# Ternary weights w1 and w2 from one ScalarE sign instead of a ScalarE relu and a VectorE clip

## The chip, the cores and the metric
One core of one Trainium2 chip runs the whole program. The metric is device time in microseconds (us), the median of three runs of the kernel. Beside it stands one execution taken by the hardware profiler; all rows below come from that one.

## What is computed
The input x is 2 x 2048 x 512 in float32. One layer attends from x to a context of 128 rows (8 heads), adds the projected result times a gate, and applies a feed-forward part with ternary weights `w_fc` (2048 x 512) and `w_proj` (512 x 2048) and a squared relu. A second layer mixes each row with `W` and applies a feed-forward part whose weights w1 (2048 x 512) and w2 (512 x 2048) are ternary too. For the change only this matters, from the second feed-forward part:

```python
def weight_quant(w):
    scale = 1.0 / jnp.clip(jnp.mean(jnp.abs(w)), 1e-05)
    q = jnp.clip(jnp.round(w * scale), -1.0, 1.0) / scale
    return w + jax.lax.stop_gradient(q - w)
```

The kernel holds w1 and w2 as the integers -1, 0 and 1 in 8-bit floats and puts the scale into the row factors of the activations. The clip of an integer to [-1, 1] and its sign are the same number.

## The kernel before, in words
The rows of x go through the kernel in 16 groups of 256 (`GROUPS`), each in two tiles of 128. TensorE does all products and, at the start, transposes of weights; ScalarE does exp, gelu, squares, copies and the high halves of split operands; VectorE does maxima, norms, drains of PSUM and the low halves; GpSimd (POOL) does low halves and adds; SyncE issues the loads and the transposing DMAs.

The order of the work is written out by hand: for each engine a table (`ORDER` for what is done per group, `PREP` for what is done once) gives each operation its place in that engine's sequence, and the engine goes through the places in turn. Between engines there are only semaphores. An engine that waits holds up all that stands behind it.

The weights are made ready once, in the first 200 us, between the operations of groups 0, 1 and 2. For w1 and w2 this goes in eight pieces of 128 x 2048 float32 (four of w1, then four of w2), after a first pass over the same data that takes their mean:

- SyncE loads piece n (n = 0 to 7) into one of two places, both in the tile `h` (`load`, lines 599 and 601). A load waits until the piece that was there has been used (`used`).
- VectorE rounds it in place: times the inverse mean, plus MAGIC (12582912.0), which leaves MAGIC plus an integer (`round_weights`, line 1158, semaphore `c_round`).
- ScalarE lifts it: relu of the piece plus (1 - MAGIC), that is max(integer + 1, 0), into a bf16 buffer `lifted[n % 2]`, which lies in `hT` (line 932, `c_lift`). From n = 2 on it waits until clip n - 2 has left the buffer.
- VectorE clips it: min with 2, minus 1, as an 8-bit float into `w1T` or `w2T` (`clip_weights`, line 1173, `c_clip`). Before the first piece of w1 it waits for the products that read `w1T`'s memory as another weight (`c_cps`), before the first of w2 for the split of `wx` (`c_whi`, `c_wlo`), whose source lies in `w2T`.

TensorE waits for `c_clip` at its first product with w1 (4 pieces) and with w2 (8 pieces), SyncE at the first transpose into `hT` (8 pieces). The similar weights `w_fc` and `w_proj` are made by TensorE transposes and a ScalarE Sign from PSUM with the bias `drop` = -MAGIC (line 874).

Other lines that the prediction speaks of: 1365 (VectorE, the low half of a split, here of probabilities `p`, queries and attention output `qT`), 1391, 1395 and 1399 (VectorE: row maximum, bias of the exp, inverse of the sum), 949 (ScalarE exp), 957 (ScalarE, high half of the probabilities), 971 and 975 (ScalarE, the low-rank path to `tlow`), 985, 990 and 996 (ScalarE, drain of the first feed-forward part: relu and squares), 1130 (VectorE, low half of `wx`), 1417 (VectorE, residual after attention), 1430 (VectorE, remainder of the low-rank path), 759 and 764 (POOL, low half of the hidden values, and norm of the probabilities), 617 (SyncE, transposing DMA of `p` into `pt`), 1758 (TensorE, probabilities times values), 1818, 1844, 1887 and 1903 (TensorE: up, down, w1, w2).

Of the kernel before, what the change touches and what calls it, by code (L numbers as in the profile page):

```python
# [19 lines left out]
ACT = mybir.ActivationFunctionType  # L20
# [3 lines left out]
P = 128  # L24
# [24 lines left out]
def build(nc, x_d, ctxT_d, wqT_d, wkvT_d, woT_d, wfc_d, wproj_d, uT_d, wxT_d, wcT_d, bx_d, w1T_d, b1_d, w2T_d, b2_d,  # L49
          rope_d, small_d, out_d):  # L50
    ctx = ExitStack()
    with ctx:
# [32 lines left out]
        lift = sb("lift", [P, 1], F32)  # L85
# [140 lines left out]
        def mix_bank(g, n):  # L226
# [15 lines left out]
        lifted = [hT[:, t, :, :].rearrange("p c n -> p (c n)").bitcast(BF16) for t in range(TILES)]  # L242
# [18 lines left out]
         c_scps, c_sc, c_asum, c_asumps, c_mean, c_round, c_lift, c_clip) = [sem(n) for n in (  # L261
# [4 lines left out]
            "c_asumps c_mean c_round c_lift c_clip").split()]  # L266
# [55 lines left out]
        def used(eng, n):  # L322

            if n < SUM0:
                eng.wait_ge(c_tern, KC * (n + 1))
            elif n < W0:
                eng.wait_ge(c_asum, n - SUM0 + 1)
            else:
                eng.wait_ge(c_lift, n - W0 + 1)

        def last_in(place):
# [49 lines left out]
                rot_lo=((26, 28), (68, 71), (112, 113), (164, 165), (213, 214), (263, 264), (310, 311), (357, 360),  # L381
                        (409, 410), (457, 458), (505, 506), (553, 554), (604, 605), (653, 654), (703, 704),
                        (751, 752)),
                rot=((19, 21), (65, 66), (110, 111), (160, 163), (210, 212), (259, 260), (306, 307), (356, 358),
                     (407, 408), (453, 454), (503, 504), (551, 552), (600, 601), (649, 650), (701, 702), (744, 745)),
                sum=((35, 38, 42, 43), (77, 84, 85, 93), (118, 120, 130, 135), (168, 172, 179, 181),
# [3 lines left out]
                max=((30, 32, 33, 37), (74, 75, 78, 79), (115, 116, 121, 122), (166, 167, 170, 173),  # L390
# [3 lines left out]
                p_lo=((40, 41, 46, 49), (83, 89, 95, 96), (127, 136, 137, 141), (174, 178, 186, 187),  # L394
# [3 lines left out]
                pv=((53, 54), (99, 101), (144, 145), (191, 192), (239, 240), (290, 291), (338, 339), (386, 387),  # L398
                    (433, 434), (484, 486), (536, 537), (584, 585), (634, 635), (681, 683), (730, 731), (779, 780)),
                x1=((57, 59), (105, 106), (149, 150), (195, 196), (247, 248), (294, 295), (342, 344), (390, 391),  # L400
                    (439, 440), (491, 492), (540, 541), (588, 591), (639, 640), (687, 688), (737, 738), (783, 787)),
                ln2=((58, 64), (108, 109), (152, 153), (197, 198), (250, 251), (297, 298), (346, 347), (392, 393),
                     (445, 446), (496, 497), (546, 547), (593, 595), (644, 645), (689, 690), (739, 741), (784, 791)),
                low=((82,), (117,), (159,), (207,), (258,), (308,), (355,), (403,), (455,), (507,), (555,), (603,),
                     (651,), (697,), (749,), (796,)),
                q4=((123, 126), (171, 176), (215, 233), (262, 279), (317, 322), (363, 378), (411, 431), (463, 474),
                    (516, 521), (565, 576), (614, 619), (658, 665), (708, 716), (757, 766), (795, 798), (819, 821)),
                x3=((119, 124), (162, 175), (211, 221), (257, 272), (312, 321), (361, 375), (405, 422), (459, 468),
                    (513, 520), (558, 566), (606, 615), (655, 664), (699, 713), (753, 765), (793, 797), (818, 820)),
                h=((131, 132, 133, 134, 138, 139, 143, 147), (180, 183, 184, 185, 188, 190, 202, 206),  # L410
# [7 lines left out]
                q5_sc=((140, 156), (189, 208), (238, 253), (289, 303), (334, 352), (384, 404), (432, 450),  # L418
                       (483, 499), (534, 545), (580, 596), (631, 646), (680, 691), (726, 746), (775, 786),
                       (803, 809), (828, 833)),  # L420
                q5=((142, 158), (193, 209), (241, 256), (292, 305), (340, 359), (389, 406), (437, 452), (485, 502),
                    (538, 548), (583, 599), (632, 647), (682, 700), (736, 748), (781, 788), (805, 812), (832, 834)),
                x4=((154, 169), (203, 216), (254, 266), (304, 316), (351, 369), (399, 416), (451, 462), (500, 515),
                    (550, 562), (598, 609), (642, 657), (692, 705), (747, 758), (790, 794), (816, 824), (835, 836)),
                ln3=((104, 107), (148, 161), (199, 204), (246, 261), (301, 309), (343, 354), (388, 402), (438, 456),
                     (490, 501), (544, 557), (590, 602), (638, 652), (686, 696), (732, 750), (785, 792), (811, 815)),
                x2=((100, 103), (146, 157), (194, 200), (237, 255), (293, 302), (341, 353), (385, 397), (436, 449),
                    (487, 498), (539, 549), (587, 597), (637, 648), (684, 694), (725, 740), (782, 789), (810, 813)),
                ln1_st=((0, 1), (10, 12), (60, 61), (125, 151), (177, 201), (223, 249), (280, 296), (333, 345),
                        (376, 396), (426, 441), (469, 493), (527, 542), (567, 592), (623, 641), (685, 695),  # L430
                        (727, 728)),
                ln1=((2, 3), (11, 15), (63, 69), (128, 155), (182, 205), (227, 252), (288, 300), (335, 348),
                     (383, 398), (435, 444), (480, 495), (532, 543), (572, 594), (633, 643), (693, 698), (733, 734))),
# [99 lines left out]
            DVE=dict(x3lo_end=(814, 817), ctx_sum=(14,), rot_k=(8, 9), wq_max=(4,), wq_scale=(5,), k_max=(16,),  # L533
# [3 lines left out]
                     wx_lo=(88,), row_scale=(62,), mean=(70,), diag=(56,), round=(72, 73, 81, 86, 90, 91, 98, 102),  # L537
                     clip=(76, 80, 87, 92, 94, 97, 114, 129)),
# [40 lines left out]
        def _(sp):  # L579
# [260 lines left out]
        def _(act):  # L840
# [18 lines left out]
            def evac(q):  # L859

                kind, i = QUANT[q]
                if q == 0:
                    act.wait_ge(c_const, 6)
# [217 lines left out]
        def _(dve):  # L1081
# [78 lines left out]
            def clip_weights(n):  # L1160
# [827 lines left out]
```

## Time and profile before

| | us |
|---|---|
| median of 3 runs | 1144.55 (1144.29 to 1144.96) |
| the profiled execution: its own time | 1145.46 |
| its span in the profile | 1143.4 |
| TensorE busy | 1086.2 (95%) |
| VectorE busy | 923.9 (81%) |
| ScalarE busy | 798.3 (70%) |
| GpSimd busy | 584.6 (51%) |

The span goes from the first to the last instruction that the profiler recorded; the execution's own time has 2.1 us around it. Busy time is the time in which an engine had an instruction under way, and says nothing of whether others waited for it.

### The profile page before, as it was taken

What the parts mean: (1) busy time and instruction counts of PE and PEld (TensorE: products, weight loads), DVE (VectorE), ACT (ScalarE), POOL (GpSimd) and SP (SyncE); (2) the same over time, 40 slices, a digit from 0 to 9 for tenths busy, and PEclk for the clock granted to TensorE, in tenths of its full rate; (3) what the DMA queues carried; (4) which work ended last, traced back from release to release, by engine and by line L of the source; (5) the groups of instructions that cost most, each with busy time, mean ns of one, the idle gap of its engine ahead of it and who ended that gap; (6) DMA issues with size and microseconds to landing.
All of it is one profiled execution on the core that took longest, in us unless ns stands there. A gap on an engine that the chain in (4) does not pass through costs nothing.

```text
span 1143.4 us, 22172 instructions
## 1 busy us (share of the span) xinstructions
PE 1086.2 (95%) x8270; PEld 676.6 (59%) x8558; DVE 923.9 (81%) x1989; ACT 798.3 (70%) x1575; POOL 584.6 (51%) x567
## 2 busy tenths in 40 slices
PE   5776799999999999999999999999999999999997
PEld 5544556475756656474756656565756666564744
DVE  3786788988788797878889888888878777988676
ACT  3988957677685949485876849495775868595634
POOL 1442646564655655556546457463546466564421
PEclk9988799999999999999999999999999999999998
DMA  9779751452534443433335245334343254333110
GB/s 335 239 241 317 232 147 41 95 130 65 120 79 103 98 105 86 100 82 87 93 83 139 61 112 97 86 101 87 89 99 99 54 109 114 75 93 74 38 47 28
DMA packets 273802, 128.11 MB, mean 112 GB/s; under 512 B 247568, under 2 KB 248080, under 8 KB 272016
## 3 DMA queue, kind: packets, MB, share of 16 engines
q1 hardware_dynamic: 273136, 125.73, 43.6%
q8 instruction: 67, 1.10, 0.4%
q10 hardware_dynamic: 560, 0.96, 0.3%
q14 instruction: 39, 0.32, 0.1%
HBM read 57.19 MB, written 8.39 MB: 57 GB/s over the span
## 4 chain that ended last, share of the span: by engine, by line
PE 86%; DMA 4%; ACT 3%; DVE 3%; issue 1%; SPq 1%; POOL 1%; ACTq 0%; DVEq 0%
PE ps L1844 19%; PE ps L1818 18%; PE ps L1887 10%; PE ps L1903 9%; PE ps L1866 7%; PE ps L1771 6%; PE ps L1718 6%; PE ps L1824 2%; PE ps L1758 2%; PE ps L1743 2%; DMA w1T<-in_wcT 1%; PE ps L1611 1%; DMA hT<-q 1%; PE ps L1683 1%; PE ps L1660 1%
## 5 line engine op out<-in xcount | busy, mean ns | idle before, releaser
L1818 PE MATMUL ps<-xT,fcT 128*128 128x256 f16 x2048 | 259.1, 274 | 8.2 <-DMA xT<-x16f 3.9
L732 POOL TENSOR_TENSOR rs<-ve,nhalf 128x1 f32<-128x1 f32 x160 | 102.1, 643 | 283.1 <-DVE ve L1357 207.9
L1844 PE MATMUL ps<-pjT,hid 128*128 128x512 fp8e4 x1024 | 232.1, 379 | 0.0
L1818 PEld LDWEIGHTS ps<-xT,fcT 128*128 128x128 fp8e4 x2048 | 199.1, 98 | 47.1 <-issue 6.5
L759 POOL TENSOR_TENSOR hid<-sq,hid 128x512 f16<-128x512 f32 x128 | 158.6, 1246 | 49.8 <-ACT sq L996 49.3
L1844 PEld LDWEIGHTS ps<-pjT,hid 128*128 128x128 f16 x1024 | 98.3, 98 | 98.9
L949 ACT ACTIVATE e<-ps,nmb,sig 128x128 f32<-128x128 f32 x256 | 113.0, 458 | 7.9 <-DVE nmb L1395 7.8
L985 ACT ACTIVATE rl<-ps,rsf 128x256 f32<-128x256 f32 x256 | 106.5, 469 | 15.6 <-PE ps L1824 14.9
L1887 PE MATMUL ps<-w1T,q4T 128*128 128x512 fp8e4 x480 | 113.4, 379 | 0.0
L764 POOL TENSOR_TENSOR e<-e,einv 128x512 f32<-128x512 f32 x64 | 71.0, 1116 | 74.2 <-DVE einv L1399 73.9
L1903 PE MATMUL ps<-w2T,hT 128*128 128x512 fp8e4 x480 | 108.6, 379 | 0.3 <-DMA hT<-q 0.3
L1503 DVE SCALAR_TENSOR_TENSOR h<-ps,dqs,b1bc 128x512 f32<-128x512 f32 x120 | 86.4, 743 | 21.1 <-PE ps L1887 19.8
L1041 ACT ACTIVATE q<-h 128x2048 f16<-128x2048 f32 x30 | 57.2, 1908 | 55.3 <-DVE h L1514 55.3
L1718 PE MATMUL ps<-pt,wq 128*128 128x256 f16 x768 | 88.2, 275 | 3.6 <-DMA pt<-x16a 2.7
L1771 PE MATMUL ps<-wo,qT 128*128 128x512 f16 x384 | 85.6, 379 | 1.0 <-DVE qT L1365 1.0
L1718 PEld LDWEIGHTS ps<-pt,wq 128*128 128x128 f16 x768 | 75.4, 99 | 16.9 <-DMA pt<-x16a 3.5
L990 ACT ACTIVATE hid<-rl 128x512 f16<-128x512 f32 x128 | 80.7, 630 | 5.0
L1866 PE MATMUL ps<-wx,xT 128*128 128x512 f16 x360 | 82.4, 379 | 1.4 <-DVE r L1539 1.3
L1083 DVE TENSOR_REDUCE amax<-h 128x1 f32<-128x2048 f32 x30 | 68.5, 2282 | 15.3 <-ACT h L1010 15.3
L996 ACT ACTIVATE sq<-rl 128x512 f32<-128x512 f32 x128 | 78.5, 613 | 0.0
L1903 PEld LDWEIGHTS ps<-w2T,hT 128*128 128x128 f16 x480 | 45.9, 98 | 50.6
L1824 PE MATMUL ps<-tlow,lowA 128*128 128x256 bf16 x256 | 68.2, 273 | 0.1
(243 smaller groups left out, 1987.6 us busy)
## 6 DMA issues: line engine op xcount, KB each, us to landing
xb<-in_x SPq DMA_DIRECT2D x16, 512.0 KB, 4.3
xa<-in_x SPq DMA_DIRECT2D x15, 512.0 KB, 3.9
out<-r SPq DMA_DIRECT2D x30, 256.0 KB, 2.3
rope<-in_rope SPq DMA_DIRECT2D x16, 384.0 KB, 3.5
h<-in_w1T SPq DMA_DIRECT2D x6, 1024.0 KB, 6.4
h<-in_w2T SPq DMA_DIRECT2D x6, 1024.0 KB, 5.9
hid<-in_w_fc SPq DMA_DIRECT2D x2, 1024.0 KB, 8.7
h<-in_wkvT SPq DMA_DIRECT2D x2, 1024.0 KB, 10.3
```

The source lines that it names most:

```text
L732: pool.tensor_tensor(rs[:, n, t:t + 1], ve[:, n, t:t + 1], nhalf[:, :], ALU.pow).then_inc(done, 1)
L759: pool.tensor_tensor(flat[:, 1, :], sq[:, m % 2, :], flat[:, 0, :], ALU.subtract).then_inc(hid_lo, 1)
L949: last = act.activation(e[:, n, a * S:(a + 1) * S], s_bank(g, n)[:, a * S:(a + 1) * S], ACT.Exp, bias=nmb[:, n, a:a + 1], scale=sig[:, :], ...
L985: act.activation(rl[:, m % 2, a * G:(a + 1) * G], ps[:, FFN0 + m % 2, a * G:(a + 1) * G], ACT.Relu, scale=rsf[:, 2 * m + a:2 * m + a + 1]) ...
L1718: mm = pe.matmul(q_bank(hg)[:, a * G:(a + 1) * G], wq[:, ws, k, c:c + P], xT1[:, xs, k, :], start=(n == 0 and k == 0), stop=(n == 2 and k ...
L1771: mm = pe.matmul(wo_bank(t), ao[:, xs, k, t * P:(t + 1) * P], wo[:, ws, k, :], start=(n == 0 and k == 0), stop=(n == 2 and k == KC - 1))
L1818: pe.matmul(ps[:, FFN0 + m % 2, a * G:(a + 1) * G], fcT[:, k, f * P:(f + 1) * P], xT2[:, xs, k, :], start=(xs == 0 and k == 0), stop=False)
L1824: return pe.matmul(ps[:, FFN0 + m % 2, a * G:(a + 1) * G], lowA[:, f * P:(f + 1) * P], tlow[:, :], start=False, stop=True)
L1844: mm = pe.matmul(ps[:, FFN0 + t, :], hid[:, xs, c, t * P:(t + 1) * P], pjT[:, c, :], start=(c == 0 and xs == 0), stop=(c == FC - 1 and xs ...
L1866: mm = pe.matmul(mix_bank(g, t), xT3_of(g)[:, xs, k, t * P:(t + 1) * P], wx[:, ws, k, :], start=(n == 0 and k == 0), stop=(n == 2 and k == ...
L1887: mm = pe.matmul(mix_bank(g, 2 + u), q4T_of(g)[:, k, t * P:(t + 1) * P], w1T[:, k, n * 512:(n + 1) * 512], start=(k == 0), stop=(k == KC - 1))
L1903: mm = pe.matmul(mix_bank(g, 10 + t), hT_of(g)[:, t, c, :], w2T[:, c, :], start=(c == 0), stop=(c == FC - 1))
```

## The change
Piece n is still rounded by VectorE. ScalarE then takes the sign of (piece - MAGIC) and writes it straight into `w1T` or `w2T`; VectorE's clip, the buffers `lifted`, the constant `lift` and the wait of ScalarE for the clip are gone. The waits that stood before the clips of pieces 0 and 4 now stand before ScalarE's signs of these pieces, and the waits for `c_clip` are waits for `c_tern12`, which the sign raises; SyncE's first transpose into `hT` waits for the mean's sums (`used(sp, last_in(4))`) instead. The places in VectorE's table are renumbered without the eight clips, and nothing else in them changes its turn; the tables of the other engines are as they were.

```diff
-                    if n >= 2:
-                        act.wait_ge(c_clip, n - 1)
+                    kind, i = LOADS[W0 + n]
+                    if kind == "w1":
+                        if i == 0:
+                            act.wait_ge(c_cps, BATCH)
+                        dst = w1T[:, i, :]
                     else:
-                        used(act, last_in(4))
-                    act.activation(lifted[n % 2], piece[PLACE[W0 + n]], ACT.Relu, bias=lift[:, :]).then_inc(c_lift, 1)
+                        if i == 0:
+                            act.wait_ge(c_whi, 3)
+                            act.wait_ge(c_wlo, 3)
+                        dst = w2T[:, 4 * i:4 * i + 4, :].rearrange("p c n -> p (c n)")
+                    act.activation(dst, piece[PLACE[W0 + n]], ACT.Sign, bias=drop[:, :], saturate=False).then_inc(c_tern12, 1)
...
-            def clip_weights(n):
-
-                kind, i = LOADS[W0 + n]
-                dve.wait_ge(c_lift, n + 1)
-                if kind == "w1":
-                    if i == 0:
-                        dve.wait_ge(c_cps, BATCH)
-                    dst = w1T[:, i, :]
-                else:
-                    if i == 0:
-                        dve.wait_ge(c_whi, 3)
-                        dve.wait_ge(c_wlo, 3)
-                    dst = w2T[:, 4 * i:4 * i + 4, :].rearrange("p c n -> p (c n)")
-                dve.tensor_scalar(dst, lifted[n % 2], 2.0, 1.0, ALU.min, ALU.subtract, saturate=False)\
-                    .then_inc(c_clip, 1)
...
-                for n in here("DVE", "clip", p):
-                    clip_weights(n)
...
-            pool.memset(lift[:, :], 1.0 - MAGIC).then_inc(c_const, 1)
...
                 if first(g) and t == 0:
-                    sp.wait_ge(c_clip, 8)
+                    used(sp, last_in(4))
                 need(sp, w2_ps, TILES, g - 1, t)
```

## Rows read from the trace of the kernel before

**Rows 1.** The page: busy time, share of the span and instructions of each engine.

```profile
PE 1086.2 (95%) x8270; PEld 676.6 (59%) x8558; DVE 923.9 (81%) x1989; ACT 798.3 (70%) x1575; POOL 584.6 (51%) x567
```

**Rows 2.** Busy time by stretch: PE, PEld, DVE, ACT, POOL (instructions), clock, DMA share, GB/s.

```profile
107.90:144.40 36.50, 23.90 (x252) 18.39 (x253) 26.14 (x35) 35.41 (x76) 20.38 (x14) 0.72 0.80 244
144.40:181.00 36.60, 34.94 (x300) 19.60 (x309) 28.50 (x51) 17.98 (x29) 15.68 (x15) 1.00 0.51 130
181.00:1080.00 899.00, 895.28 (x6953) 554.67 (x7208) 750.34 (x1636) 635.72 (x1271) 497.94 (x479) 1.00 0.40 91
```

**Rows 3.** TensorE's waits, 117 to 220 us: total us, times, longest.

```profile
PE ps L1818 <- DVE tres L1430: 2.5, 2, 1.7
...
PE ps L1718 <- DVE r L1417: 0.9, 1, 0.9
PE ps L1771 <- DVE qT L1365: 0.5, 1, 0.5
```

**Rows 4.** All waits of ScalarE, 107.9 to 152.3 us.

```profile
ACT rl L985 <- PE ps L1824: 0.6, 1, 0.6
ACT lowsum L971 <- PE ps L1784: 0.3, 1, 0.3
```

**Rows 5.** Groups by line and form, first 200 us: busy us, mean ns | idle before.

```profile
L949 ACT ACTIVATE e<-ps,nmb,sig 128x128 f32<-128x128 f32 x43 | 19.0, 460 | 0.0
...
L932 ACT ACTIVATE hT<-h,lift 128x2048 bf16<-128x2048 f32 x8 | 15.9, 1994 | 0.0
...
L874 ACT ACTIVATE pjT<-ps,drop 128x512 fp8e4<-128x512 f32 x16 | 10.1, 685 | 1.4 <-PE ps L1611 1.4
...
L924 ACT ACTIVATE h<-h 128x2048 f32<-128x2048 f32 x4 | 7.6, 1905 | 4.1 <-DMA h<-in_w2T 4.1
...
L1173 DVE TENSOR_SCALAR w2T<-hT 128x2048 fp8e4<-128x2048 bf16 x4 | 6.6, 1652 | 1.6 <-ACT hT L932 1.6
L1173 DVE TENSOR_SCALAR w1T<-hT 128x2048 fp8e4<-128x2048 bf16 x4 | 6.5, 1637 | 0.0
...
L904 ACT ACT_TABLE_LOAD x1 | 1.3, 1283 | 2.2 <-issue 2.2
```

**Rows 6.** The chain of waits, 133 to 156 us: start, us, what.

```profile
133.11 1.89 ACT hT L932
...
138.81 0.53 ACT p L957
...
139.36 1.24 DVE p L1365
...
140.62 3.65 DMA pt<-p
...
145.25 10.51 PE ps L1844 x48
```

**Rows 7.** ScalarE's instructions in time: start, us, line, count, idle before.

```profile
114.33 3.88 ACT L932 ACTIVATE hT<-h,lift 128x2048 bf16<-128x2048 f32 x2
...
126.53 2.04 ACT L932 ACTIVATE hT<-h,lift 128x2048 bf16<-128x2048 f32 x1
```

**Rows 8.** VectorE's instructions in time, 120 to 199 us.

```profile
120.00 0.18 DVE L1399 RECIPROCAL einv<-esum 128x4 f32<-128x4 f32 x1 [1.09 <-ACT e L949]
...
124.95 0.42 DVE L1430 TENSOR_TENSOR tres<-ps,tlow 128x256 f32<-128x256 f32 x1 [0.40 <-ACT tlow L975]
...
139.36 1.23 DVE L1365 TENSOR_TENSOR p<-e,p 128x512 f16<-128x512 f32 x1 [5.78 <-ACT p L957]
...
178.64 0.69 DVE L1391 TENSOR_REDUCE nmx<-ps 128x4 f32<-128x512 f32 x1 [1.64 <-PE ps L1743]
...
198.75 2.06 DVE L1173 TENSOR_SCALAR w2T<-hT 128x2048 fp8e4<-128x2048 bf16 x1
```

**Rows 9.** GpSimd's instructions in time, 127 to 148 us.

```profile
127.34 4.09 POOL L764 TENSOR_TENSOR e<-e,einv 128x512 f32<-128x512 f32 x2 [6.05 <-DVE einv L1399]
...
146.97 1.04 POOL L764 TENSOR_TENSOR e<-e,einv 128x512 f32<-128x512 f32 x1
```

More of the change, by code:

```diff
@@ L84, in build @@
         nhalf = sb("nhalf", [P, 1], F32)
-        lift = sb("lift", [P, 1], F32)
         xa = sb("xa", [P, TILES, D], F32)
@@ L241, in build @@
         ktmp = rl[:, :, :]
-        lifted = [hT[:, t, :, :].rearrange("p c n -> p (c n)").bitcast(BF16) for t in range(TILES)]
         vT_sb = small[:, 0:KC * RANK].rearrange("p (k r) -> p k r", k=KC)
@@ L260, in build @@
          c_tern, c_quantp, c_lowps, c_low, c_lowzero, c_lowF, c_lowt, c_lowact, c_bnd, c_rsf, c_scd,
-         c_scps, c_sc, c_asum, c_asumps, c_mean, c_round, c_lift, c_clip) = [sem(n) for n in (
+         c_scps, c_sc, c_asum, c_asumps, c_mean, c_round, c_tern12) = [sem(n) for n in (
             "d_ctx d_wv d_kr d_wq d_wo d_wx d_wc d_small d_rows d_u d_b1 c_const c_kps c_vps c_kru c_krot "
@@ L265, in build @@
             "c_lowps c_low c_lowzero c_lowF c_lowt c_lowact c_bnd c_rsf c_scd c_scps c_sc c_asum "
-            "c_asumps c_mean c_round c_lift c_clip").split()]
+            "c_asumps c_mean c_round c_tern12").split()]
         d_piece = [sem(f"d_piece{n}") for n in range(5)]
@@ L328, in used @@
             else:
-                eng.wait_ge(c_lift, n - W0 + 1)
+                eng.wait_ge(c_tern12, n - W0 + 1)
         def last_in(place):
@@ L380, in build @@
             DVE=dict(
[L381 to L385, printed above, removed]
@@ L400, in build @@
[L400 to L405, printed above, removed]
@@ L406, in build @@
[L406 to L410, printed above, removed]
[7 rows of a table removed]
@@ L418, in build @@
[L418 to L433, printed above, removed]
+                rot_lo=((26, 28), (68, 71), (106, 107), (156, 157), (205, 206), (255, 256), (302, 303), (349, 352),
+                        (401, 402), (449, 450), (497, 498), (545, 546), (596, 597), (645, 646), (695, 696),
+                        (743, 744)),
@@ new lines, in build @@
+                rot=((19, 21), (65, 66), (104, 105), (152, 155), (202, 204), (251, 252), (298, 299), (348, 350),
+                     (399, 400), (445, 446), (495, 496), (543, 544), (592, 593), (641, 642), (693, 694), (736, 737)),
+                sum=((35, 38, 42, 43), (76, 82, 83, 89), (111, 113, 122, 127), (160, 164, 171, 173),
[3 rows of a table added]
+                max=((30, 32, 33, 37), (74, 75, 77, 78), (108, 109, 114, 115), (158, 159, 162, 165),
[3 rows of a table added]
+                p_lo=((40, 41, 46, 49), (81, 86, 90, 91), (120, 128, 129, 133), (166, 170, 178, 179),
[3 rows of a table added]
@@ new lines, in build @@
+                pv=((53, 54), (93, 95), (136, 137), (183, 184), (231, 232), (282, 283), (330, 331), (378, 379),
+                    (425, 426), (476, 478), (528, 529), (576, 577), (626, 627), (673, 675), (722, 723), (771, 772)),
+                x1=((57, 59), (99, 100), (141, 142), (187, 188), (239, 240), (286, 287), (334, 336), (382, 383),
+                    (431, 432), (483, 484), (532, 533), (580, 583), (631, 632), (679, 680), (729, 730), (775, 779)),
+                ln2=((58, 64), (102, 103), (144, 145), (189, 190), (242, 243), (289, 290), (338, 339), (384, 385),
+                     (437, 438), (488, 489), (538, 539), (585, 587), (636, 637), (681, 682), (731, 733), (776, 783)),
@@ new lines, in build @@
+                low=((80,), (110,), (151,), (199,), (250,), (300,), (347,), (395,), (447,), (499,), (547,), (595,),
+                     (643,), (689,), (741,), (788,)),
+                q4=((116, 119), (163, 168), (207, 225), (254, 271), (309, 314), (355, 370), (403, 423), (455, 466),
+                    (508, 513), (557, 568), (606, 611), (650, 657), (700, 708), (749, 758), (787, 790), (811, 813)),
+                x3=((112, 117), (154, 167), (203, 213), (249, 264), (304, 313), (353, 367), (397, 414), (451, 460),
+                    (505, 512), (550, 558), (598, 607), (647, 656), (691, 705), (745, 757), (785, 789), (810, 812)),
@@ new lines, in build @@
+                h=((123, 124, 125, 126, 130, 131, 135, 139), (172, 175, 176, 177, 180, 182, 194, 198),
[7 rows of a table added]
+                q5_sc=((132, 148), (181, 200), (230, 245), (281, 295), (326, 344), (376, 396), (424, 442),
+                       (475, 491), (526, 537), (572, 588), (623, 638), (672, 683), (718, 738), (767, 778),
+                       (795, 801), (820, 825)),
+                q5=((134, 150), (185, 201), (233, 248), (284, 297), (332, 351), (381, 398), (429, 444), (477, 494),
+                    (530, 540), (575, 591), (624, 639), (674, 692), (728, 740), (773, 780), (797, 804), (824, 826)),
@@ new lines, in build @@
+                x4=((146, 161), (195, 208), (246, 258), (296, 308), (343, 361), (391, 408), (443, 454), (492, 507),
+                    (542, 554), (590, 601), (634, 649), (684, 697), (739, 750), (782, 786), (808, 816), (827, 828)),
+                ln3=((98, 101), (140, 153), (191, 196), (238, 253), (293, 301), (335, 346), (380, 394), (430, 448),
+                     (482, 493), (536, 549), (582, 594), (630, 644), (678, 688), (724, 742), (777, 784), (803, 807)),
+                x2=((94, 97), (138, 149), (186, 192), (229, 247), (285, 294), (333, 345), (377, 389), (428, 441),
+                    (479, 490), (531, 541), (579, 589), (629, 640), (676, 686), (717, 732), (774, 781), (802, 805)),
@@ L434, in build @@
+                ln1_st=((0, 1), (10, 12), (60, 61), (118, 143), (169, 193), (215, 241), (272, 288), (325, 337),
+                        (368, 388), (418, 433), (461, 485), (519, 534), (559, 584), (615, 633), (677, 687),
+                        (719, 720)),
+                ln1=((2, 3), (11, 15), (63, 69), (121, 147), (174, 197), (219, 244), (280, 292), (327, 340),
+                     (375, 390), (427, 436), (472, 487), (524, 535), (564, 586), (625, 635), (685, 690), (725, 726))),
             ACT=dict(
@@ L532, in build @@
                     row_scale=(27,), mean=(30,), spread=(1, 10, 12, 15, 26)),
-            DVE=dict(x3lo_end=(814, 817), ctx_sum=(14,), rot_k=(8, 9), wq_max=(4,), wq_scale=(5,), k_max=(16,),
+            DVE=dict(x3lo_end=(806, 809), ctx_sum=(14,), rot_k=(8, 9), wq_max=(4,), wq_scale=(5,), k_max=(16,),
                      wq_lo=(7,), v_max=(17,), kv_scale=(23,), k_lo=(27,), v_lo=(31, 36), low_copy=(22,),
@@ L536, in build @@
                      mix_row=(51,), low_rank=(39,), v_parts=(52,), wx_max=(50,), hidden=(55,), wx_scale=(67,),
-                     wx_lo=(88,), row_scale=(62,), mean=(70,), diag=(56,), round=(72, 73, 81, 86, 90, 91, 98, 102),
-                     clip=(76, 80, 87, 92, 94, 97, 114, 129)),
+                     wx_lo=(85,), row_scale=(62,), mean=(70,), diag=(56,), round=(72, 73, 79, 84, 87, 88, 92, 96)),
             ACT=dict(q4_end=(549, 550), wq=(5,), k_hi=(18,), v_hi=(20, 21), tanh=(1,), wo=(19,),
@@ L722, in _ @@
             pool.memset(nhalf[:, :], -0.5).then_inc(c_const, 1)
-            pool.memset(lift[:, :], 1.0 - MAGIC).then_inc(c_const, 1)
             pool.memset(drop[:, :], -MAGIC).then_inc(c_const, 1)
-            pool.wait_ge(c_const, 5)
+            pool.wait_ge(c_const, 4)
             pool.affine_select(out=ident[:, :], in_=ident[:, :], compare_op=ALU.not_equal, fill=1.0, base=0,
@@ L862, in evac @@
                 if q == 0:
-                    act.wait_ge(c_const, 6)
+                    act.wait_ge(c_const, 5)
                 if q == 4:
@@ L1102, in spread_diag @@
                 if n == 0:
-                    dve.wait_ge(c_const, 6)
+                    dve.wait_ge(c_const, 5)
                 else:
@@ L1183, in v_parts @@
                                          ALU.subtract).then_inc(c_vrep, 1)
-                dve.wait_ge(c_const, 6)
+                dve.wait_ge(c_const, 5)
                 dve.tensor_reduce(fold1[:, :], ident[:, :].rearrange("p (a r) -> p r a", r=RANK), axis=AX.X, op=ALU.add)\
@@ L1191, in low_rank @@
             def low_rank():
-                dve.wait_ge(c_const, 6)
+                dve.wait_ge(c_const, 5)
                 dve.tensor_copy(identb[:, :], ident[:, :])
@@ L1600, in ternary @@
                     pe.wait_ge(c_kru, 6)
-                    pe.wait_ge(c_const, 6)
+                    pe.wait_ge(c_const, 5)
                 if kind == "fc":
@@ L1872, in w1_up @@
                 if first(g) and u == 0:
-                    pe.wait_ge(c_clip, 4)
+                    pe.wait_ge(c_tern12, 4)
                 ring = 3
@@ L1892, in w2_down @@
                 if first(g) and t == 0:
-                    pe.wait_ge(c_clip, 8)
+                    pe.wait_ge(c_tern12, 8)
                 need(pe, h_done, 4 * TILES, g, t + 5)
```

5 lines of the change are left out of this document (removed), and 32 rows, old and new, of tables (h, max, p_lo, sum).

## The prediction

> **What bounds the kernel now.** I read the page first. TensorE is busy 95% of the span, VectorE 81%, ScalarE 70% [rows 1]. These are averages, and the change touches only the stretch in which w1 and w2 are made, so the busy times by stretch came second [rows 2]. There are three stretches to tell apart. From 107.9 to 144.4 us TensorE works 23.9 of 36.5 us, VectorE 26.1, and ScalarE 35.4: ScalarE is the bound there, at 97%. From 144.4 to 181 TensorE works 34.9 of 36.6 us, from 181 to 1080 895.3 of 899: from 144.4 on TensorE is the bound, at a granted clock of 1.00 (the upper level). So the third view to read is who waits, TensorE first and then ScalarE. From 117 to 220 us TensorE waits on VectorE for the low-rank remainder (2.5 us, two times), a residual (0.9) and a split of attention output (0.5) [rows 3]. None names the clip on line 1173; its one other large wait, 1.8 us, is for relu drains on ScalarE. ScalarE waits only 0.9 us in all between 107.9 and 152.3, both times for TensorE [rows 4], and never for a clip, though its line 932 has that wait from the third piece on. Last, the chain of waits shows how the first stretch hands over to the second: ScalarE's lift of piece 3, then relu drains (not shown), the high half of p (138.81), its low half on VectorE (139.36), the transposing DMA (140.62 to 144.27), then TensorE, which runs 48 matmuls at a stretch at 145.25 [rows 6].
>
> **The change part by part.**
>
> *The eight clips go.* They are 6.6 + 6.5 = 13.1 us of VectorE, at 1.64 us each on average, and with them goes 1.6 us in which VectorE waited for lifts [rows 5]. What they are worth depends on what stands behind each on VectorE. Clip 0 took 1.22 us, and the next instruction began at 120.00 after 1.09 us of waiting for ScalarE's exp [rows 8]: without the clip it waits 2.3 us. Clips 1 and 2 (122.08 and 128.60) come before the 5.78 us that VectorE waits for ScalarE's high half of p, up to 139.36: hidden. In front of the remainder on line 1430, for which TensorE waits 1.7 us, VectorE itself waited 0.40 us for ScalarE's `tlow` [rows 8], so clip 1 did not hold that either. Clips 3, 4 and 5 (143.81, 146.98, 152.30) stand where TensorE has its matmuls in one run [rows 6], and VectorE meets it again at 155.86, after waiting 0.5 us for it. Clip 6 (175.78) ends 1.64 us before VectorE gets scores from TensorE at 178.64 [rows 8]. That wait ends with TensorE and not with VectorE, and the 0.8 us that TensorE then waits for a remainder follow from there. Clip 7 (198.75, 2.06 us) is the only one with no wait of note behind it: after it come the drains of the first products with w1. TensorE shows no wait for those drains [rows 3]: a wait for line 1503 would stand in that view. The value of the removal on the path is therefore 0. What is late next where a clip goes is, each time, ScalarE or TensorE.
>
> *The lift becomes a sign.* Both read 128 x 2048 float32 from SBUF with a bias column; only the function and the output type (8-bit float for bf16) differ. The lift takes 1.99 us [rows 5]. A Sign from SBUF with 8-bit output is not in the trace, so I bound it. From above: the Sign that makes `w_proj` ternary takes 0.685 us for 128 x 512 from PSUM [rows 5], so four of those, 2.74 us, or 0.75 more than a lift. An exp of only 128 elements a lane takes 0.46 us already [rows 5], so much of that excess is a start cost paid four times. From below: the sums over the same pieces (an Abs with no bias column) take 1.905 us [rows 5], 0.08 less. The nearest row is the lift itself, same engine, source, size and bias form: 1.99 us, difference 0. The price on the path if it differs by d, for d above 0: pieces 0 and 1 (114.33, together) have 0.3 us of waiting behind them, piece 2 (126.53) has 0.6 [rows 4, 7], piece 3 has none and stands in the chain [rows 6], and pieces 4 to 7 lie beside TensorE's full stretch. So 2d - 0.3, plus d - 0.6, plus d, each no less than 0: for d = 0.75 that is 1.2 + 0.15 + 0.75 = 2.1 us. For d = -0.08 the gain is at most 4 x 0.08 = 0.3 us.
>
> The Trainium skill has a sentence on this, "ScalarE: Activation LUTs", section "What ACT_TABLE_LOAD costs": an activation with a bias column takes some 1990 ns at 2048 elements a lane, whatever the function. The lifts' 1994 ns agree, no row here shows it for a Sign of that size, and by it d is 0.
>
> *The waits move.* The sign of piece 0 now waits for products that ended at 71 us, 43 us before. The sign of piece 4 (144.96 before) waits for the low half of `wx`, which ended at 133.6 and comes earlier without clip 2. Behind these waits on ScalarE stand the exps and the relu drains, but neither wait holds. The dropped wait of lift n for clip n - 2 held nothing [rows 4]. Loads of later pieces wait for the lift, now for the sign, at the same point of ScalarE's order: the load of piece 7 at 152.94 follows lift 5 and the transposes ahead of it on SyncE's queue, as before. TensorE's waits for four and eight pieces are met at about 147 and 166 us instead of 146 and 201, before use at 195.9 and 221.1. The rounds can start earlier by the clips ahead of them, 1.2 us for piece 2, but then wait for the same loads and for the same lifts ahead of them: 0. A memset of one column (0.1 us) goes at the start, where nothing waits for GpSimd: 0.
>
> *The port.* Two norms on GpSimd took 4.09 us together at 127.34, beside a round and a clip on VectorE, and one took 1.04 us at 146.97 [rows 9]; the split of p on the chain took 1.24 us with GpSimd at work [rows 6]. So VectorE and GpSimd slow each other, and fewer VectorE instructions give GpSimd time back. On the path it buys nothing, since GpSimd's results are then waited for by nobody, and the split at 139.36 meets a GpSimd instruction started by ScalarE at 138.8, which does not move.
>
> The Trainium skill, "SBUF — State Buffer", section "Who interferes with whom", makes it a lock that one of the two holds for a whole instruction. Rows 9 agree in direction (2.04 against 1.04 us for each norm). By the rule up to 13.1 us of lock time go, which is what the second case below would live on.
>
> The sum: 0 for the clips, 0 for the signs, 0 for the waits, 0 for the port. The profiled execution took 1145.46 us, 0.9 above the median of 1144.55; I put the sum of 0 on the median and forecast **1144.5 us**. Removing work from a fixed order can't delay anything by itself; a delay can only come from a dearer sign, a new table load, or a change in who meets whom at the port.
>
> **The rivals.**
>
> *A, the forecast:* time unchanged within 0.7 us either way, 1143.8 to 1145.2.
>
> *B, the freed VectorE time reaches the path.* The most it can buy is all of the waiting that I have put down to others but that VectorE or GpSimd might shorten: 0.9 us on ScalarE [rows 4] and TensorE's waits for VectorE after 144.4, 0.9 + 0.8 + 0.5 [rows 3], together 3.1 us: 1141.4. Half of it, 1143.0, is what I would expect if a port meeting resolves the other way. For it: the slow norms, the 1.24 us split. Against: ScalarE is 97% busy and keeps all of its work.
>
> *C, the other side: the sign is dearer than the lift.* Place: ScalarE between 114 and 139 us. Price: as worked out, up to +2.1 us, 1146.6. It decides from a sign of 2.0 us upward for piece 3 alone, from 2.15 us for pieces 0 and 1 too. For it: 0.685 us for 512 elements. Against: that row is a PSUM read with its own start cost.
>
> *D, the sign needs another activation table.* A load takes 1.28 us [rows 5]. If Sign were not in the table in use, loads would come before piece 0, before the exps behind piece 1, before piece 2, and before the exps at 179.6. The first two cost 2.57 - 0.3, the third 1.28 - 0.6, the last is hidden in a wait: 3.0 us slower, 1147.5, or +0.26%. Against it: in the first 200 us there are 43 exps and 32 Signs mixed, and the only table load is the one at the start [rows 5]. The page "ScalarE: Activation LUTs" of the Trainium skill, section "Table sets: the hidden batching unit", states the rule behind this case: the functions of one set are to be run together, and each switch costs a load. The rows say that Sign and exp share one here.
>
> That the change does not do what it says would show as VectorE's busy time not falling; the diff leaves no room for it.
>
> **How the numbers follow.** What a measurement of this kernel can tell from no change is about 0.2%, 2.3 us, so the bounds are 1142.3 and 1146.8. A 0.82, B 0.10, C 0.05, D 0.03. Faster by more than 0.2% is most of the upper part of B and a little of A: 0.06. Slower by more is D and the end of C: 0.05. Within: 0.89. The range reaches from most of B, 1142.8, to most of C, 1146.2.
>
> **What would show it.** ScalarE's line for w1T and w2T at 1.99 us x 8 (A and B), above 2.1 (C), a table load between 110 and 180 us (D). VectorE busy 13 us less, at about 911 us. The waits of VectorE for ScalarE's exps and high halves longer by the clips before them. TensorE's run of 48 matmuls starting at 145.25 within 0.3 us, and its busy time in the whole unchanged at 1086. The norms on GpSimd at 127 us shorter than 2 us each. The prediction is wrong if that run starts over 1 us earlier or later, or if TensorE's waits after 181 us, 3.7 us up to 1080 now [rows 2], change by over 1 us.

## The result and the profile after

| | before | after |
|---|---|---|
| median, us (20 runs each; lowest to highest) | 1144.56 (1141.37 to 1148.54) | 1146.86 (1143.46 to 1150.45) |
| the profiled execution: own time / span | 1145.46 / 1143.4 | 1148.77 / 1146.8 |

The ratio is 1.0021, 95% interval [1.0013, 1.0029]: 2.3 us slower, where no change was forecast. The profiled execution lies 1.9 us above its median, the one of before 0.9 above its own, so the two traces are 3.3 us apart and the medians 2.3. A single trace can lie 2 or 3 us off its kernel's median, so the traces below are read for mechanisms and the medians and ratios for the size.

First the page's busy line of the changed kernel, which answers to [rows 1]:

```profile
PE 1084.1 (95%) x8270; PEld 676.0 (59%) x8558; DVE 911.3 (79%) x1981; ACT 798.7 (70%) x1575; POOL 581.3 (51%) x566
```

VectorE does eight instructions and 12.6 us less, as it should. The three stretches of the changed kernel, columns as in [rows 2]:

```profile
107.90:144.40 36.50, 25.40 (x256) 19.37 (x258) 22.03 (x32) 35.06 (x75) 17.39 (x12) 0.69 0.77 234
144.40:181.00 36.60, 34.94 (x301) 19.61 (x306) 22.69 (x47) 18.06 (x29) 14.88 (x15) 1.00 0.55 129
181.00:1080.00 899.00, 891.24 (x6918) 551.55 (x7171) 746.18 (x1632) 631.99 (x1265) 497.46 (x479) 1.00 0.44 91
```

In the first two, where the change works, TensorE is as busy as before or busier, and the loss is not there. It is in the third, where not one instruction was changed: TensorE is busy 891.24 us there instead of 895.28, 4.0 less. In the same stretch the share of time in which the DMA engines were busy rose from 0.40 to 0.44, while the rate stayed at 91 GB/s. More time for the same bytes: that is the first hint.

The signs, among the groups of the first 200 us (busy, mean ns | idle before), answer to the lifts and the table load of [rows 5]:

```profile
L934 ACT ACTIVATE w2T<-h,drop 128x2048 fp8e4<-128x2048 f32 x4 | 8.0, 1988 | 0.0
L934 ACT ACTIVATE w1T<-h,drop 128x2048 fp8e4<-128x2048 f32 x4 | 7.9, 1999 | 0.0
...
L900 ACT ACT_TABLE_LOAD x1 | 1.3, 1283 | 2.2 <-issue 2.2
```

TensorE's waits from 175 to 1090 us (total, times, longest), the largest first. This is the view that tells where the 4 us went:

```profile
PE ps L1887 <- DMA hT<-q: 3.7, 5, 1.0
PE ps L1850 <- DVE r L1523: 1.4, 1, 1.4
PE ps L1777 <- ACT lowsum L973: 0.9, 2, 0.5
PE ps L1802 <- DVE tres L1414: 0.7, 1, 0.7
PE ps L1755 <- DVE qT L1349: 0.5, 1, 0.5
PE ps L1727 <- DVE qT L1349: 0.3, 1, 0.3
PE ps L1742 <- DMA pt<-p: 0.3, 1, 0.3
```

The same view of the kernel before:

```profile
PE ps L1866 <- DVE r L1539: 1.3, 1, 1.3
PE ps L1793 <- ACT lowsum L971: 1.0, 2, 0.5
PE ps L1818 <- DVE tres L1430: 0.7, 1, 0.7
PE ps L1771 <- DVE qT L1365: 0.5, 1, 0.5
PE ps L1743 <- DVE qT L1365: 0.3, 1, 0.3
PE ps L1903 <- DMA hT<-q: 0.3, 1, 0.3
```

The other waits have their counterparts (TensorE's line numbers are 16 lower after). One has grown: the product with w2 waits for the transposing DMA of the quantized hidden values `q5` into `hT` five times and 3.7 us in all, before once and 0.3 us. (The rows leave the numbers of buffers out: `q` is `q5`.)

So the DMAs next, from 181 to 1080 us: the data queue (packets, MB, share of 16 engines), then each kind with its count, KB for plain ones, and median us from issue to landing. Before:

```profile
q1 hardware_dynamic: 233264, 80.90, 39.2%
...
xb<-in_x SPq DMA_DIRECT2D x14, 512.0 KB, 4.3
...
pt<-p SPq DMA_TRANSPOSE x56, 2.8
q4T<-x16b SPq DMA_TRANSPOSE x30, 2.3
hT<-q SPq DMA_TRANSPOSE x28, 3.7
xT<-x16b SPq DMA_TRANSPOSE x28, 2.8
```

After:

```profile
q1 hardware_dynamic: 233264, 80.90, 43.9%
...
xb<-in_x SPq DMA_DIRECT2D x14, 512.0 KB, 4.3
...
pt<-p SPq DMA_TRANSPOSE x56, 3.2
q4T<-x16b SPq DMA_TRANSPOSE x30, 2.5
hT<-q SPq DMA_TRANSPOSE x28, 4.3
xT<-x16b SPq DMA_TRANSPOSE x28, 3.2
```

### The profile page after: what moved, and what is told of

It is laid out like the page before. It is cut to its first block, busy times and chain, and to the rows that moved or that the text cites. A ratio compares the mean times of both kernels' runs of the same rounds, so it can differ in the third digit from the quotient of the medians.

```text
span 1146.8 us, 22155 instructions
## 1 busy us (share of the span) xinstructions
PE 1084.1 (95%) x8270; PEld 676.0 (59%) x8558; DVE 911.3 (79%) x1981; ACT 798.7 (70%) x1575; POOL 581.3 (51%) x566
## 4 chain that ended last, share of the span: by engine, by line
PE 79%; ACT 8%; DMA 6%; DVE 3%; issue 1%; SPq 1%; POOL 1%; ACTq 0%; DVEq 0%
PE ps L1828 16%; PE ps L1802 15%; PE ps L1887 9%; PE ps L1871 9%; PE ps L1850 6%; PE ps L1702 6%; PE ps L1755 6%; DMA hT<-q 3%; PE ps L1742 2%; PE ps L1808 2%; PE ps L1727 1%; ACT e L951 1%; ACT q L1043 1%; ACT rl L987 1%; DMA w1T<-in_wcT 1%
## 5 line engine op out<-in xcount | busy, mean ns | idle before, releaser
L755 POOL TENSOR_TENSOR hid<-sq,hid 128x512 f16<-128x512 f32 x128 | 155.9, 1224 | 52.6 <-ACT sq L998 52.2
L1349 DVE TENSOR_TENSOR p<-e,p 128x512 f16<-128x512 f32 x64 | 53.0, 844 | 24.2 <-ACT p L959 24.1
```

The source lines that it names most:

```text
L755: pool.tensor_tensor(flat[:, 1, :], sq[:, m % 2, :], flat[:, 0, :], ALU.subtract).then_inc(hid_lo, 1)
```

## The experiments

**Theory (addresses):** the loss comes from the place of tiles in memory; put back, it is gone, with VectorE's work still removed. **Rival (traffic):** it comes from the changed order of work in the first 200 us or from VectorE's other timing, which moves DMAs against each other; then it stays whatever the addresses are. Each ratio below is against the kernel before on the same chip, whose median was 1144.83 us for the first four kernels, 1144.97 for the second four, and 1145.13 for the last three. "Start" is the address of the tiles `xa` to `hT` past a multiple of 256, as the built program of each run lists it. The ratios come with their intervals and are not the quotients of the medians shown: in the run at start 128 that quotient is 1.0023, the ratio 1.0034, and in run 7 1.0018 and 1.0025.

**1. The changed kernel with the 32 bytes back.**

```diff
+        gap = sb("gap", [P, 8], F32)
         xa = sb("xa", [P, TILES, D], F32)
```

> The changed kernel with an unused column of 32 bytes where the column `lift` was, so that every tile from `xa` on has the address it had before the change (a multiple of 256 bytes). Theory A (addresses: without `lift` these tiles start 32 bytes lower, at 224 past a multiple of 256, and the transposing DMAs take longer): the slowdown is gone, ratio to the kernel before 1.000 +- 0.0007, pt<-p 2.8 us and hT<-q 3.7 us to landing, TensorE's waits for hT 0.3 us. Theory B (order: the freed VectorE time and the direct signs shift who meets whom): the gap changes nothing, ratio 1.002, hT<-q stays at 4.3 us.

Measured: 1145.6 us, ratio 1.0004 [0.9993, 1.0015]. The DMAs from 181 to 1080 us:

```profile
q1 hardware_dynamic: 233264, 80.90, 39.1%
...
pt<-p SPq DMA_TRANSPOSE x56, 2.8
...
hT<-q SPq DMA_TRANSPOSE x28, 3.7
```

Every kind of transpose takes what it took before, TensorE waits 0.5 us for `hT`, and it is busy 894.55 us in the stretch. The same instructions in the same order, an unused tile more, and the loss is gone. This is also the change without its side effect: no measurable difference.

**2. The kernel before, with `lift` declared last.** All its work stays, VectorE's clips too; only the addresses are those of the changed kernel.

```diff
-        lift = sb("lift", [P, 1], F32)
         xa = sb("xa", [P, TILES, D], F32)
...
         pad = sb("pad", [P, 1], F32)
+        lift = sb("lift", [P, 1], F32)
```

> The kernel before with all its clips, only `lift` is declared last, so that the tiles from `xa` on start 32 bytes lower, as in the changed kernel. Theory A: slower by what the changed kernel is, ratio 1.002 (1.0013 to 1.0029), hT<-q 4.3 us, pt<-p 3.2 us. Theory B: ratio 1.000, hT<-q 3.7 us.

Measured: 1147.99 us, ratio 1.0023 [1.0009, 1.0037], the queue's share 44.4%, `hT<-q` at 4.3 us, four waits for it of 2.0 us in all. The kernel before gets the whole loss without the change (its trace shows less of it than its medians; this trace lies 2.3 us below its median). With run 1 this leaves no measurable part for traffic.

**3, 4, 5. Which addresses?** The changed kernel with other gaps before `xa`: 24 columns of F32 (start 64), 40 columns (start 128), 72 columns (a multiple of 512).

> The changed kernel with a gap of 96 bytes, which puts the tiles from `xa` on at 64 past a multiple of 256 bytes. Under theory A it tells which multiple counts: if 64 bytes is enough, ratio 1.000 and pt<-p 2.8 us; if it has to be 256 bytes, ratio 1.002 and pt<-p 3.2 us. Theory B: ratio 1.002 as the changed kernel.

> The changed kernel with a gap of 160 bytes: the tiles from `xa` on at 128 past a multiple of 256 bytes. If reading a source costs more wherever it does not start at a multiple of 256 (theory A256): long times, pt<-p 3.2 and hT<-q 4.3 us, share of the data queue near 44% from 181 to 1080 us, ratio 1.002 to 1.004. If a multiple of 128 is enough (A128): short times, 2.8 and 3.7 us, share 39%, ratio 1.000.

> The changed kernel with a gap of 288 bytes: the tiles from `xa` on at a multiple of 512 bytes (256 past one in the kernel before). If 256 is the multiple that counts, as in run e1: ratio 1.000, times as in e1 (pt<-p 2.8, hT<-q 3.7 us). If a larger multiple helps further, this is the version that beats the kernel before: shorter transposes and ratio under 0.999.

| start | gap, bytes | us | ratio | `hT<-q`, us | share | TensorE waits for `hT`, us |
|---|---|---|---|---|---|---|
| 224 (the change) | 0 | 1146.86 | 1.0021 [1.0013, 1.0029] | 4.3 | 43.9% | 3.7 |
| 64 | 96 | 1149.33 | 1.0039 [1.0025, 1.0054] | 4.3 | 43.6% | 3.5 |
| 128 | 160 | 1147.63 | 1.0034 [1.0023, 1.0045] | 4.3 | 43.7% | 2.8 |
| 0 (of 512: 256) | 32 | 1145.60 | 1.0004 [0.9993, 1.0015] | 3.7 | 39.1% | 0.5 |
| 0 (of 512: 0) | 288 | 1144.78 | 1.0004 [0.9991, 1.0017] | 3.7 | 39.1% | 0.8 |

Multiples of 64 and of 128 are not enough, a multiple of 512 gives nothing over one of 256. `hT<-q` (4.3) and `pt<-p` (3.2) are the same at 224, 64 and 128, and the packets of 256 bytes take 23.2, 22.8 and 22.9 ns on average, against 20.1 and 20.0 in the two runs at 0. The ratios at 64 and 128 (six runs each) look a little larger than at 224; their intervals overlap it, and whether there is more to it stays open.

**6. Source or target?** Sources (`x16a`, `x16f`, `x16b`, `p16`, `q5`) at 0, targets (`pt`, `xT2`, `xT3`, `q4T`, `hT`) at 224.

```diff
+        gap = sb("gap", [P, 8], F32)
         xa = sb("xa", [P, TILES, D], F32)
...
+        gap2 = sb("gap2", [P, 56], F32)
         pt = ...
...
+        hT = sb("hT", [P, TILES, FC, P], F16)
+        gap3 = sb("gap3", [P, 8], F32)
         qT = ...
```

> The changed kernel with `xa` and all sources of transposes (x16a, x16f, x16b, p16, q5) back at multiples of 256 bytes, and only the targets of transposes (pt, xT2, xT3, q4T, hT) at 224 past one. Theory A, if writing off the multiple costs: all transposes at the long times (pt<-p 3.2, hT<-q 4.3 us), ratio 1.002; if reading does: short times, ratio 1.000. Theory B: ratio 1.002 with short times.

Measured: 1144.95 us, ratio 1.0002 [0.9989, 1.0015]; share 39.6%, `hT<-q` 3.7, `pt<-p` 2.8 us, 20.4 ns for a packet of 256 bytes. The target's place costs nothing that can be seen here. It is the source that has to start at a multiple of 256 bytes.

**7, 8. Which of the transposes costs the time?** All of them got longer; TensorE shows a wait for one. Run 7 has all tiles at 0 but `q5` at 224 (56 columns before `q5`, 8 columns before `hT`, 8 before `xa`). Run 8 is its complement, all at 224 but `q5` and `hT` at 0:

```diff
+        gap = sb("gap", [P, 8], F32)
         q5 = ...
```

> The changed kernel with every tile back at a multiple of 256 bytes except q5, the source of hT, at 224 past one. If the slowdown comes through hT alone (theory Q: TensorE waits for hT in five places): hT<-q 4.3 us, all other transposes short, ratio 1.002. If it takes all transposes together, because each shares the queue on SyncE with the others (theory S): ratio under 1.001.

> The changed kernel with its tiles 32 bytes low, as it is, except q5 and hT, which are back at a multiple of 256 bytes. Theory Q: ratio 1.000, hT<-q 3.7 us with pt<-p still at 3.2. Theory S: over 1.001, and TensorE's waits for hT stay over 1.5 us since the transposes ahead of it on the queue are late.

| | us | ratio | `hT<-q` / `pt<-p`, us | waits for `hT` | TensorE busy 181 to 1080 |
|---|---|---|---|---|---|
| 7: only `q5` off | 1147.07 | 1.0025 [1.0015, 1.0035] | 4.3 / 2.8 | 3.3 us, 5 | 891.85 |
| 8: only `q5` on | 1145.40 | 1.0005 [0.9997, 1.0014] | 3.7 / 3.2 | 1.1 us, 2 | 893.98 |

The DMA rows of run 7 and then of run 8:

```profile
q1 hardware_dynamic: 233264, 80.90, 41.0%
...
pt<-p SPq DMA_TRANSPOSE x56, 2.8
...
hT<-q SPq DMA_TRANSPOSE x28, 4.3
```

```profile
q1 hardware_dynamic: 233264, 80.90, 42.5%
...
pt<-p SPq DMA_TRANSPOSE x56, 3.2
...
hT<-q SPq DMA_TRANSPOSE x28, 3.7
```

Read the two against each other. Run 8 has most of the added DMA time (42.5% against 39.1%) and none of the measurable loss; run 7 has less of it (41.0%) and all of the loss. What counts is which transfer has a waiter: 28 transposes of `q5`, each 0.6 us longer, of which five made TensorE wait up to 0.9 us. That the other 168 came later cost nothing that run 8 can tell from 0 (1.0005 [0.9997, 1.0014]).

**9. One piece of w1 on VectorE.** From 108 to 144 us ScalarE is the bound and VectorE has time, now more than before. With the addresses of run 1, piece 3 gets neither a round nor a sign: VectorE makes it from the loaded weights by two comparisons with half the mean.

```diff
+            def compare_weights(n):
...
+                dve.tensor_scalar(dst, src, winv1[:, 0:1], -0.5, ALU.mult, ALU.is_lt, saturate=False).then_inc(c_less, 1)
+                dve.wait_ge(c_less, 1)
+                dve.scalar_tensor_tensor(dst, src, half[:, 0:1], dst, ALU.is_gt, ALU.subtract, saturate=False).then_inc(c_tern12, 1)
```

> The changed kernel at the old addresses (a used column `half` stands where `lift` was), with piece 3 of w1 made ternary by two VectorE comparisons and without its round and its ScalarE sign: the sign that stands in the chain at 133 us goes. If ScalarE bounds the stretch from 108 to 144 us, as read from its 35.4 busy of 36.5 us: TensorE's run of 48 matmuls starts 0.8 to 1.9 us earlier, at 143.3 to 144.3, with 2.3 us more of VectorE's time; ratio 0.9985 to 0.9993. If something else stands right behind ScalarE (the transposing DMA of p, or TensorE's own products): under 0.3 us earlier, ratio 1.000.

Measured: 1143.17 us, ratio 0.9986 [0.9977, 0.9995]: faster than the kernel before, by 0.14%. TensorE's timeline (start, us, line, count) in run 9, the same two places in run 1, then VectorE's in run 9:

```profile
108.88 0.60 PE L1705 MATMUL ps<-wsum,ones 128*128 128x8 f32 x2 [6.79 <-ACT hT L921]
...
142.73 10.53 PE L1845 MATMUL ps<-pjT,hid 128*128 128x512 fp8e4 x48
```

```profile
108.18 0.60 PE L1689 MATMUL ps<-wsum,ones 128*128 128x8 f32 x2 [6.70 <-ACT hT L921]
...
142.82 10.53 PE L1829 MATMUL ps<-pjT,hid 128*128 128x512 fp8e4 x48
```

```profile
127.28 1.76 DVE L1172 TENSOR_SCALAR w1T<-h,winv 128x2048 fp8e4<-128x2048 f32 x1 [1.38 <-ACT w1T L937]
129.08 2.35 DVE L1174 SCALAR_TENSOR_TENSOR w1T<-h,half,w1T 128x2048 fp8e4<-128x2048 f32 x1
```

The traces reach the product for the mean, which lies ahead of everything that was changed, at times more than 2 us apart (108.18 in run 1, 110.50 in the kernel before). So the start of the 48 matmuls has to be counted from it: 33.85 us in run 9, 34.64 in run 1, which has the same addresses and all eight signs on ScalarE, and 34.72 in the kernel before (110.50 to 145.22 in its timeline). 0.8 us of the 2.0 us sign come back as time, the lower end of what was expected. (In the changed kernel it is 35.08, 109.98 to 145.06; TensorE's granted clock from 107.9 to 144.4 us was 0.69 there and 0.78 in run 1.) The rest of the 1.96 us between the medians (1143.17, 1145.13) is not placed.

**10, 11. Another 2 us off ScalarE's bound.** The high half of `wx` (line 845, 1.99 us) stands ahead of TensorE's products on ScalarE. I moved it behind them, with its low half on VectorE: to place 73.5 (from 53) and 89.5 (from 85), once on top of run 9 and once alone on run 1.

```diff
-                     wx=(53,), ...
+                     wx=(73.5,), ...
...
-                     wx_lo=(85,), ...
+                     wx_lo=(89.5,), ...
```

> As e9, and ScalarE's high half of wx (2.0 us at 112 us) and VectorE's low half of it (3.1 us) stand behind 144 us, where ScalarE waits much. If ScalarE bounds the stretch: the first products of the up part start 2 us earlier (116.9 for 118.9), the run of 48 matmuls 2.5 to 4 us earlier than in e1, ratio 0.9965 to 0.998. If the later sign of piece 4, which then waits for the split of wx, delays the relu drains before TensorE has used up its 48 matmuls: part or all is given back, ratio 0.999 to 1.001.

> The changed kernel at the old addresses with only the split of wx moved behind 144 us; all eight signs on ScalarE. ScalarE-bound theory: 1.5 to 2.2 us earlier at the run of 48 matmuls, ratio 0.998 to 0.9988. Otherwise ratio 1.000. It separates the part of wx in e10 from that of the piece.

Measured: 1147.58 us, 1.0022 [1.0012, 1.0032] on top of run 9, and 1149.67 us, 1.0041 [1.0027, 1.0055] alone: a miss, and the wrong sign. ScalarE's timeline in run 11 shows how:

```profile
114.45 4.09 ACT L935 ACTIVATE w1T<-h,drop 128x2048 fp8e4<-128x2048 f32 x2 [2.35 <-DVE h L1161]
...
145.31 1.99 ACT L845 ACTIVATE wx<-w2T,winv 128x2048 f16<-128x2048 f32 x1
149.90 2.00 ACT L935 ACTIVATE w2T<-h,drop 128x2048 fp8e4<-128x2048 f32 x1 [2.60 <-DVE wx L1133]
151.81 0.61 ACT L960 ACTIVATE p<-e 128x512 f16<-128x512 f32 x1
...
152.80 0.83 ACT L988 ACTIVATE rl<-ps,rsf 128x256 f32<-128x256 f32 x2
```

Two things went wrong. First, the 2.0 us that ScalarE saved ahead of the signs did not come through: in both runs it then waited 2.35 us for VectorE's round of piece 0, where run 1 has no such wait and run 9 one of 0.5. Counted from the product for the mean, the 48 matmuls begin 0.4 us earlier in run 10 than in run 9 (33.43 for 33.85) and 1.0 us later in run 11 than in run 1 (35.60 for 34.64). What stood right behind ScalarE here was VectorE's round; the rounds of pieces 0 and 1 took 4.3 us together in these two runs, 2.7 in run 1.

Second, the sign of piece 4 overwrites the memory that `wx` is split from and waits 2.60 us for the low half. Behind it on ScalarE stands the last relu drain of the group, which then begins at 152.80, and TensorE's second half of the down product needs it. In run 10 the 48 matmuls are no longer one run:

```profile
141.55 5.35 PE L1845 MATMUL ps<-pjT,hid 128*128 128x512 fp8e4 x24
149.83 7.04 PE L1845 MATMUL ps<-pjT,hid 128*128 128x512 fp8e4 x24 [2.93 <-issue]
```

The view names no releaser for the pause, but TensorE goes on 0.1 us after the drain has ended, in run 10 (149.72, 149.83) as in run 11 (153.63, 153.74). The pause cost more than its 2.93 us: the second 24 matmuls took 7.04 us for 5.35, at a granted clock of 0.68 from 149.8 to 153.3 and 0.84 from 153.3 to 157, so for a part of both stretches at the lower of its two levels.

```profile
149.80:153.30 3.50, 3.47 (x11) 1.43 (x14) 1.23 (x1) 3.50 (x4) 1.16 (x1) 0.68 0.95 295
```

At the next product (probabilities times values) run 10 is 4.4 us behind run 9, counted from the product for the mean (48.68 for 44.31), and the medians are 4.4 us apart. In the kernel before, this drain had 1.8 us to spare (end 148.6, need 150.4). Moving the sign of piece 4 behind the drain as well should take the second loss away and would leave the first; it was not tried.

## Why the prediction was wrong, point by point

- *The clips' removal is worth 0 on the path*: right. VectorE is 12.6 us less busy (911.3, as forecast), its wait for ScalarE's high half of p grew from 5.78 to 8.36 us and the one for the exp from 1.09 to 1.56 where 2.3 was expected, and run 1, which is the change with its old addresses, measures 1.0004 [0.9993, 1.0015].
- *The sign costs what the lift costs*: right, 1988 and 1999 ns against 1994 [rows 5]. The Trainium skill says in "ScalarE: Activation LUTs", section "What ACT_TABLE_LOAD costs": with a bias column, some 1990 ns at this size whatever the function. The traces now show it for a relu and a Sign. Rival C falls. So does D: in the first 200 us there is one table load, at the start, as before. (Over the whole program there are 28 in both kernels, the others at gelus and exps of later groups.)
- *The run of 48 matmuls starts at 145.25 within 0.3 us*: right, 145.06, but with some luck. In run 1, the same instructions at the old addresses, it starts at 142.82, which would have counted as "over 1 us earlier" and so as wrong, only because that execution reached the product for the mean 2.3 us earlier. Counted from there it is 34.72 us before, 35.08 after and 34.64 in run 1: no gain of rival B's kind can be seen.
- *The waits that move hold nothing*: right here. Run 11 shows what the wait of piece 4's sign for `wx` would cost if its cover went: 2.60 us.
- *The norms on GpSimd shorter than 2 us each*: wrong. In GpSimd's timeline after, the two took 5.10 us together, 4.09 before [rows 9]:

```profile
126.72 5.10 POOL L760 TENSOR_TENSOR e<-e,einv 128x512 f32<-128x512 f32 x2 [5.94 <-DVE einv L1383]
```

  VectorE's low half of `wx` (3.1 us) stood at 130.46 before; without the clip of piece 2 it moved up to 127.79 and lay beside these norms. In run 1, with the same instructions in the same order, they took 3.02 us together, in run 9 2.04. So fewer VectorE instructions do not shorten them by themselves; what happens to lie beside them probably does, which no run here isolates. The run of 48 matmuls came on time all the same, and over the whole GpSimd was busy 581.3 us for 584.6.
- *"A memset of one column (0.1 us) goes at the start, where nothing waits for GpSimd: 0"*: this is the step that failed. I priced the instruction that fills the column and not the 32 bytes that it lies in. With it fell the sentence "Removing work from a fixed order can't delay anything by itself; a delay can only come from a dearer sign, a new table load, or a change in who meets whom at the port". Dropping it made all transposing DMAs longer, of these the 28 of `q5` by 0.6 us each, and TensorE waited 3.4 us more for them in the profiled execution; the medians are 2.3 us apart.
- *TensorE's waits after 181 us change by over 1 us*: this was named as what would prove the prediction wrong. The part of the stretch in which it was not busy went from 3.7 to 7.8 us. No rival had a mechanism that reaches past 200 us, so the range ended at 1146.2, 0.7 below the median. What the prediction did price, clips, signs, waits and port, came to the 0 that it gave them, as far as run 1 can tell; the loss came with the one column that it priced by its memset alone.

The cause as the runs show it: a transposing DMA takes longer when its source doesn't start at a multiple of 256 bytes. The Trainium skill has a rule that would have warned of it, in "DMA: Bandwidth & Descriptors", section "How a descriptor splits into AXI transactions": a read that doesn't start at a multiple of 256 bytes begins at the boundary below, and the bytes fetched for nothing still cost transfer units. It speaks of starts of descriptors and not of transposes. The runs agree with it in that 0 and 256 of 512 are equally good, 224, 64 and 128 are not, and it is the source that matters. They agree less in size. An estimate worked out from the page's count: a packet of 256 bytes that starts at 64, 128 or 224 takes two reads for one, and 10, 12 or 15 units of 32 bytes for 8. Measured are 22.8, 22.9 and 23.2 ns for 20.1, in that order but much closer together, and most packets (the median, 18 ns) take as long as before. No trace here shows the single reads inside a packet, so that this is the mechanism is argued, not shown.

## What to carry to other kernels

Before costing a removed or added tile at nothing, work out the addresses of the tiles behind it, and keep the sources of transposing DMAs at multiples of 256 bytes by declaration order or a gap tile. When a slowdown shows where no instruction was changed, compare the DMAs' durations at equal bytes first, and test by putting the addresses back. A transfer that got longer costs only where an engine waits for it: here 196 got longer, and TensorE was seen to wait for five of them. And compare times within a stretch from a common event ahead of the change, not from the start of the trace.

## What the hardware showed unexpectedly

- A source's start off a multiple of 256 bytes made the transposing DMA of 128 x 2048 float16 4.3 us instead of 3.7, those of `p` and `x16f` 3.2 instead of 2.8 and 2.7, that of `x16a` 3.1 for 2.7, that of `x16b` into `xT3` 3.2 to 3.5 for 2.8 and into `q4T` 2.4 or 2.5 for 2.3. The plain load of `xb` took 4.1 to 4.5 us in all runs whatever the addresses.
- The extra time lies in few packets: of those of 256 bytes 11% took 30 ns or more with the sources at 224, 0.6% with them at 0, and the median stayed at 18 ns.
- The target's start had no effect (3.7 and 2.8 us with targets at 224).
- A comparison of 128 x 2048 float32 with an 8-bit result took VectorE 1.76 us, with a second operand 2.35 us, together 4.1 us for a piece of which ScalarE's sign takes 2.0. GpSimd was at work beside both for a part of the time (until 127.96 and from 130.25), so without it they may be shorter.
- A pause of 2.93 us in TensorE's work (run 10) was followed by matmuls at the lower clock level for part of the next 7 us: 24 of them took 7.04 us instead of 5.35.
